# Turning one of seven 128-row units of each batch on VectorE and by DMAs instead of on TensorE

## What is computed

```python
q = (text_hidden @ Wq).reshape(B, T_text, 16, 128).transpose(0, 2, 1, 3)
k = (vision_tokens @ Wk)...; v = (vision_tokens @ Wv)...     # 8 key/value heads, each used twice
scores = jnp.einsum('bhtd,bhsd->bhts', q, k) / sqrt(128)
attn = jax.nn.softmax(jnp.where(mask, scores, -jnp.inf), axis=-1)
out = jnp.einsum('bhts,bhsd->bhtd', attn, v)
x = layernorm(x + out.transpose(0, 2, 1, 3).reshape(B, T_text, -1) @ Wo)
```

## Time and profile before

| | us |
|---|---|
| median of 3 runs | 1717.02 |
| lowest and highest | 1716.77, 1717.21 |
| span of the profiled execution | 1718.6 |
| busy PE, DVE, ACT, POOL in it | 1685.0, 1221.3, 937.2, 664.6 |
| mean granted clock of PE | 0.994 |

### The profile page before, as it was taken

The page is one execution under the profiler, slowest core; times in us unless marked ns, Lnnn a source line. Parts: engine busy times, 40 slices in busy tenths (PEclk is TensorE's granted clock), DMA queues, the critical chain, the costliest instruction groups (busy, mean ns, idle before and its releaser), DMA issues.

```text
span 1718.6 us, 28903 instructions
## 1 busy us (share of the span) xinstructions
PE 1685.0 (98%) x10034; PEld 1517.0 (88%) x10034; DVE 1221.3 (71%) x3377; ACT 937.2 (55%) x1717; POOL 664.6 (39%) x417
## 2 busy tenths in 40 slices
PE   7999999999999999999999999999999999999996
PEld 7998889898989898989898989989898989888985
DVE  5655676877787878777778777776878787756557
ACT  5444465656565656565656565565656565644543
POOL 1220344525243333333334343443525341355435
PEclk9999999999999999999999999999999999999998
DMA  5234643423141423333232323232324130431433
GB/s 197 81 132 130 193 95 78 70 68 81 54 97 41 90 44 88 48 86 68 62 68 63 68 63 68 70 66 77 74 61 89 52 57 12 112 114 40 121 90 95
DMA packets 102856, 140.29 MB, mean 82 GB/s; under 512 B 37022, under 2 KB 81728, under 8 KB 102592
## 3 DMA queue, kind: packets, MB, share of 16 engines
q1 hardware_dynamic: 60784, 115.47, 26.8%
q10 hardware_dynamic: 38912, 14.80, 4.0%
q0 software_dynamic: 3024, 8.26, 1.8%
HBM read 113.62 MB, written 24.89 MB: 81 GB/s over the span
## 4 chain that ended last, share of the span: by engine, by line
PE 93%; DVE 2%; issue 1%; ACT 1%; DMA 1%; POOL 0%; another core or an unknown queue 0%; POOLq 0%; SPq 0%; ACTq 0%; DVEq 0%
PE b_turn L831 17%; PE b_out L850 9%; PE b_out L851 9%; PE b_out L852 9%; PE b_score L817 9%; PE b_score L819 9%; PE b_score L818 9%; PE b_out L860 5%; PE a_bank L344 5%; PE c_gate L1513 2%; PE c_down L1540 1%; PE a_bank L370 1%; PE a_bank L395 1%; PE a_bank L424 1%; PE a_bank L417 1%
## 5 line engine op out<-in xcount | busy, mean ns | idle before, releaser
L895 ACT CAST b_pT_hi<-b_turn 125x512 fp32r<-125x512 f32 (+1 forms) x768 | 406.8, 530 | 543.0 <-PE b_turn L831 539.8
L997 DVE TENSOR_TENSOR b_pT_lo<-b_turn,b_pT_hi 125x512 fp32r<-125x512 f32 (+1 forms) x768 | 478.0, 623 | 259.7 <-ACT b_pT_hi L895 254.2
L983 DVE CUSTOM_DVE_ANT_0 b_p<-b_score,b_mask_add 128x500 f32<-128x500 f32 x672 | 451.9, 673 | 58.9 <-PE b_turn L831 24.4
L831 PEld LDWEIGHTS b_turn<-ident,b_p 128*125 128x125 f32 x2688 | 409.4, 186 | 55.2
L831 PE MATMUL b_turn<-ident,b_p 128*125 128x128 f32 x2688 | 418.1, 272 | 0.0
L901 ACT ACTIVATE b_p<-b_p,b_shift 128x1500 f32<-128x1500 f32 x224 | 347.5, 1551 | 2.1 <-DVE b_top_min L991 2.1
L850 PE MATMUL b_out<-b_pT_hi,b_c_hi 125*128 125x512 f32 (+1 forms) x768 | 346.5, 451 | 0.7 <-DVE b_pT_lo L997 0.6
L1135 POOL TENSOR_TENSOR b_oT_lo<-b_oT,b_oT_hi 128x896 fp32r<-128x896 f32 x32 | 67.6, 2112 | 624.5 <-ACT b_oT_hi L925 588.0
L851 PE MATMUL b_out<-b_pT_lo,b_c_hi 125*128 125x512 f32 (+1 forms) x768 | 280.9, 366 | 0.0
L852 PE MATMUL b_out<-b_pT_hi,b_c_lo 125*128 125x512 f32 (+1 forms) x768 | 280.5, 365 | 0.0
L817 PE MATMUL b_score<-b_cT_hi,b_q_hi 128*128 128x500 f32 x672 | 262.9, 391 | 0.0
(11 more groups left out here) (250 smaller groups left out, 2402.1 us busy)
## 6 DMA issues: line engine op xcount, KB each, us to landing
cT_in<-in_ctxT SPq DMA_DIRECT2D x32, 750.0 KB, 9.8
b_c_in<-in_ctx SPq DMA_DIRECT2D x32, 750.0 KB
q_store<-a_fold_in_or_q_stage SPq DMA_DIRECT2D x16, 896.0 KB, 4.2
q_in<-q_store SPq DMA_DIRECT2D x32, 448.0 KB, 7.1
b_rden_all<-rden_store ACTq DMA_DIRECT2D x32, 256.0 KB, 3.6
b_rden_all<-rden_store ACTq DMA_DIRECT2D x32, 192.0 KB, 3.7
b_mask_in<-in_mask SPq DMA_DIRECT2D x32, 187.5 KB, 9.4
slot_store<-c_y2T SPq DMA_DIRECT2D x35, 128.0 KB, 1.7
```

The costliest lines, as they stand in the source:

```text
L831: mm = pe.transpose(turn_bank[n % 3][0:CK, u * 128:(u + 1) * 128], p[slot % 2][:, u, c * CK:(c + 1) * CK], ident[:])
L895: act.copy(pT_hi[:, n % 3, 0:w], turn_bank[n % 3][0:CK, 0:w]).then_inc(hi_done, 1)
L983: dve.tensor_tensor_reduce(out=p[slot % 2][:, u, keys], in0=score_bank[j][:, 0:FW], in1=mask_add[:, b, keys], scale=1.0, scalar=-3.0e38, o ...
L997: dve.tensor_tensor(pT_lo[:, n % 3, 0:w], turn_bank[n % 3][0:CK, 0:w], pT_hi[:, n % 3, 0:w].bitcast(F32), ALU.subtract).then_inc(lo_done, 1)
```

## The change

In every even slot the first unit is no longer transposed by PE. In step 5 of the slot, once its exponential is done, DVE turns it in 32x32 blocks with one instruction, `turn_blocks`: out of `p` (128 rows x 1500 keys, seen as 4 x 12 blocks of 32 columns; a chunk of 125 keys is taken as 4 x 32, and four columns of padding are added) into a new tile, `by_block`. SP then issues 16 DMAs of 32 partitions x 384 floats, `move_blocks`, that put the blocks at their partitions in `keyed`. `p_round` copies the high part of the unit's 128 columns from `keyed`, before it waits for PE, and that of the other 384 from PSUM. `p_rest` subtracts in two instructions likewise, the first of which has both inputs in SBUF. `scores` waits for `turned` from the second unit of an even slot on.

To make room, `oT_lo` is written over `oT` and `c_lo` over the raw values: `c_in` goes, `c_raw` has a place for each batch of the pair, and its load waits for `pv_done` itself. SP's loads are written out instead of looped and stand in another order around the moves. At the start of `phase_c` the loads of `y2` wait for other things, and two pairs of semaphores are merged.

```diff
+QUADS = 4
+ACROSS = 32 * CH
+ROW_PAD = 4
...
+        def written_over(name, shape, dt):
+
+            return nc.alloc_sbuf_tensor_at(f"b_{name}_over", shape, dt, offset=edge[name])
...
+        oT_lo = written_over("oT", [128, XH, 2, S], F32R)
         oT_hi = sb("oT_hi", [128, XH, 2, S], F32R)
-        oT_lo = sb("oT_lo", [128, XH, 2, S], F32R)
...
+        by_block = sb("by_block", [128, QUADS, CH, 32])
...
-        c_in = sb("c_in", [CK, CH * CD])
+        keyed = sb("keyed", [128, QUADS, ACROSS])
         c_hi = sb("c_hi", [CK, 2, CH * CD], F32R)
-        c_lo = sb("c_lo", [CK, 2, CH * CD], F32R)
+        c_raw = sb("c_raw", [CK, 2, CH * CD])
+        c_lo = written_over("c_raw", [CK, 2, CH * CD], F32R)
...
-        p[0] = sb("p0", [128, UNITS[0], CTX])
+        p[0] = sb("p0", [128, UNITS[0], CTX + ROW_PAD])
...
+        BLOCKS_AT = 5
+        MOVES = 16 * QUADS * QUADS
...
+        def keyed_chunk(c):
+            return keyed[0:CK, :, 32 * c:32 * (c + 1)]
+
+        def by_blocks(ap):
+            return ap.rearrange("p (a j) -> p a j", j=32)
...
+            def load_values(i, b):
+                n = 2 * i + b
+                if n >= 2:
+                    sp.wait_ge(pv_done, 2 * CH * (n - 1))
+                if n:
+                    sp.wait_ge(c_loaded, 16 * n)
+                sp.dma_start(c_raw[:, b, :], D["ctx"][n]).then_inc(c_loaded, 16)
+
+            def move_blocks(i, b):
+
+
+                n = 2 * i + b
+                if n:
+                    sp.wait_ge(lo_done, CH * (2 * n - 1))
+                sp.wait_ge(blocks_turned, n + 1)
+                for a in range(QUADS):
+                    for r in range(QUADS):
+                        sp.dma_start(keyed[32 * r:32 * (r + 1), a, :],
+                                     by_block[32 * a:32 * (a + 1), r].rearrange("q c j -> q (c j)")).then_inc(
+                                         keyed_loaded, 16)
...
-            def loads(i, first=False):
-                load_q(i, 0)
-                load_scores(i, 0)
-                load_values(i, 0)
-                load_q(i, 1)
-                load_scores(i, 1)
-                if not first:
-                    store(i - 2)
-                residual(i - 1)
-                load_values(i, 1)
-
-            loads(1, first=True)
-            with sp.Fori(2, NPAIR) as i:
-                loads(i)
-            store(NPAIR - 2)
-            residual(NPAIR - 1)
+            for i in range(NPAIR):
+                move_blocks(i, 0)
+                if i < END:
+                    load_q(i + 1, 0)
+                    load_cT(i + 1, 0)
+                    load_mask(i + 1, 0)
+                if i:
+                    load_values(i, 1)
+                if i < END:
+                    load_q(i + 1, 1)
+                    load_cT(i + 1, 1)
+                move_blocks(i, 1)
+                if i < END:
+                    load_mask(i + 1, 1)
+                if i:
+                    store(i - 1)
+                residual(i)
+                if i < END:
+                    load_values(i + 1, 0)
...
-                for u in range(units(slot)):
+                for u in range(1 - slot % 2, units(slot)):
...
-                g, w = STEPS * i + n, 128 * units(n // CH)
-                act.wait_ge(turned, g + 1)
+                g, slot, c, w = STEPS * i + n, n // CH, n % CH, 128 * units(n // CH)
+                own = 128 * (1 - slot % 2)
                 if not (first and n < 3):
                     act.wait_ge(pv_done, g - 2)
-                act.copy(pT_hi[:, n % 3, 0:w], turn_bank[n % 3][0:CK, 0:w]).then_inc(hi_done, 1)
+                if own:
+                    if c == 0:
+                        act.wait_ge(keyed_loaded, MOVES * (2 * i + slot // 2 + 1))
+                    act.copy(by_blocks(pT_hi[:, n % 3, 0:own]), keyed_chunk(c))
+                act.wait_ge(turned, g + 1)
+                act.copy(pT_hi[:, n % 3, own:w], turn_bank[n % 3][0:CK, own:w]).then_inc(hi_done, 1)
...
-                if u == 0 and not (first and slot < 2):
+                if u == 1 - slot % 2 and not (first and slot < 2):
...
+            def turn_blocks(i, slot):
+
+
+                n = 2 * i + slot // 2
+                dve.wait_ge(exp_done, PUNITS * i + unit0[slot] + 1)
+                if n:
+                    dve.wait_ge(keyed_loaded, MOVES * n)
+                own = p[0][:, 0, :]
+                keys = bass.AP(own.tensor, own.offset, [own.ap[0], [32, QUADS], [CK, CH], [1, 32]])
+                dve.transpose(by_block[:], keys).then_inc(blocks_turned, 1)
+
             def p_rest(i, n):
-                w = 128 * units(n // CH)
+                slot, c, w = n // CH, n % CH, 128 * units(n // CH)
+                own = 128 * (1 - slot % 2)
                 dve.wait_ge(hi_done, STEPS * i + n + 1)
-                dve.tensor_tensor(pT_lo[:, n % 3, 0:w], turn_bank[n % 3][0:CK, 0:w],
-                                  pT_hi[:, n % 3, 0:w].bitcast(F32), ALU.subtract).then_inc(lo_done, 1)
+                if own:
+                    dve.tensor_tensor(by_blocks(pT_lo[:, n % 3, 0:own]), keyed_chunk(c),
+                                      by_blocks(pT_hi[:, n % 3, 0:own]).bitcast(F32), ALU.subtract)
+                dve.tensor_tensor(pT_lo[:, n % 3, own:w], turn_bank[n % 3][0:CK, own:w],
+                                  pT_hi[:, n % 3, own:w].bitcast(F32), ALU.subtract).then_inc(lo_done, 1)
...
+                    if n // CH % 2 == 0 and n % CH == BLOCKS_AT:
+                        turn_blocks(i, n // CH)
...
-            sp.wait_ge(*attention.c_split)
+            sp.wait_ge(*attention.first_batch_weighed)
+            load_y2(2)
+            sp.wait_ge(*attention.keyed_taken)
             load_y2(0)
-            sp.wait_ge(*attention.first_batch_weighed)
             load_y2(1)
-            load_y2(2)
```

81 lines of the change are left out of this document (40 added, 41 removed).

## The result

The changed kernel takes **1843.06 us** (median of 4; 1840.93 to 1846.43), the kernel before 1717.12: ratio **1.0733**, 95% interval 1.0718 to 1.0748. The forecast was 1772.6 with a range up to 1830. The direction was right, the size was not: 126 us came on top where the sum had 56, and the time lies 13 us above the range.

What follows compares the result with a forecast made beforehand. PE was taken to bound the kernel, with 93% of the chain. 1718.6 - 43.4 (transposes) + 98 (waits for GpSimd) + 1 (tail) = 1774.2 us profiled, less 1.6: 1772.6 us; range 1690 to 1830.

Steps and rivals of the forecast that it cites:

- What is removed: PE's queue: 384 transposes fewer at 0.113 us each, a gain of 43.4 us, all on PE.
- ScalarE: 384 added casts of 125x128 out of SBUF, 0.15 to 0.3 us each, hidden by the wait for PE: 0 us.
- VectorE's block transpose: One 1536-column instruction behind step 5's low part: 1.75 us, bounds 0.9 and 3.5, just fitting, not waiting for GpSimd.
- The wait for GpSimd: Low-part pieces with both inputs in SBUF wait for GpSimd's present instruction: 98 us, bounds 45 and 135.
- the walk: Steps 15 to 26 and 39 to 50 followed against GpSimd's instructions: with block-transpose lateness, 6.5 us for each of 15 pairs.
- The moves: SyncE's sixteen DMAs per batch land in time for ScalarE's cast: 0 us, upper end 1 us in each of 32 batches.
- The tail: The load of the first y2 tiles is issued later, at 1490.3 instead of 1473.5: +1 us (0 to 5).
- C: Rival: moves come late or the block transpose takes two passes, 30 to 56 us on top; 0.16 with the stalls' upper end.
- A: Rival: VectorE's pieces do not wait for GpSimd or always slip in between, 1675 us; chance 0.14.
- B: Rival: GpSimd's blocks exist but VectorE makes them up, 1 to 2.7 us a pair, 1690 to 1715 us; chance 0.08.
- the ring: Follow-up theory: late moves delay ScalarE's denominators' store, whose landing delays exponentials and VectorE's next block transpose, enlarging each lateness.

Runs made afterwards that it cites:

- e8: Changed kernel with four large moves per batch, low part's first operand from PSUM, moves ahead of the loads and the opening's last store (wrong numbers): 1680.5 us, ratio 0.9781.
- e5: Changed kernel with block transposes and sixteen moves that nobody reads, TensorE making all four transposes: 1725.4 us, ratio 1.0035.
- h2: Changed kernel with VectorE copying moved blocks into PSUM before one low part, moves ahead of the loads, block transpose at step 4: 1745.6 us, ratio 1.0159.
- e1: Changed kernel with the first operand of the seventh unit's low part from PSUM instead of SBUF (wrong numbers): 1758.2 us, ratio 1.0248.
- h1: e8 with sixteen moves per batch again in place of four (wrong numbers still): 1762.7 us, ratio 1.0272.
- f0: Changed kernel with SyncE's order alone changed: moves ahead of the q and ctxT loads and the opening's last store: 1861.7 us, ratio 1.0816.
- e6: Kernel before with only the low part split in two, the 128-column piece having both inputs in SBUF (wrong numbers): 1825.1 us, ratio 1.0627.
- e3: Changed kernel with four large moves per batch and the low part's first operand from PSUM, old order (wrong numbers): 1744.5 us, ratio 1.0160.
- e2: Changed kernel with four large moves per batch in place of sixteen (wrong numbers): 1787.3 us, ratio 1.0418.
- e9: Changed kernel with moves ahead of the loads and ScalarE copying moved blocks into PSUM for one 512-column low part: 1767.8 us, ratio 1.0307.
- f1: e9 with the block transpose one step earlier, at step 4 of the slot: 1729.0 us, ratio 1.0057.

## Why the prediction was right in direction and wrong in size

**What is removed: right.** 2304 transposes at an unchanged mean of 272 ns. The sum had -43.4; e8 has -37. The 6 us between are of the size of what e5 shows for layout, loads, block transposes and traffic together (7.8 us, with sixteen moves); no run parts them further.

**ScalarE: right.** The new cast takes 295 ns (estimate 150 to 300) and in e8 nobody waits for it.

**VectorE's block transpose: right.** 1.77 us (estimate 1.75), 1767 to 1771 ns all 32 times; 27 of the 32 ran beside a GpSimd instruction. The Trainium skill ("SBUF — State Buffer", Who interferes with whom) has it that an instruction with at most one SBUF input outside the two-port modes stays out of the contention: with h2's copy (282 to 297 ns 384 times) the traces agree.

**The wait for GpSimd: right in mechanism, the size in part by luck.** The sum had 98 us. Four pairs of runs measure it: 85 (e1 to the changed kernel), 99 (h1 to f0), 107 (e6, of which 13 fall in the first pair, which the walk left out), and only 43 where four moves come late by their place (e3 to e2). The mechanism is the one in the earlier trace rows. The places in the walk were partly others. In the changed kernel's timeline a piece begins inside `oT_lo` 31 times, inside `q_lo` 30 times and inside `c_lo` 29 times in 32 batches, 14 of these in steps 15 to 26, where the walk had it fall into the projection; inside `cT_lo` only 3 times, where the walk had 1.7 us a pair; and 15 times inside a short instruction (L1176) that the walk did not have. One error made up for the other.

**The moves: this step failed.** It took 0, with 1 us in each of 32 batches as its upper end. The runs show 78 us for the moves as they stand in the changed kernel (e8 to e1). Three things went wrong in it. (1) An issue was priced at 0.57 us from the earlier trace rows, where four stood alone; sixteen take 10.02 to 10.56, and with 1.9 to 3.6 us for the last landing the blocks are there 12 to 13 us after the transpose. The working had 10.9 to 13.4 itself, against 11.5, and let PE's 1.6 us of lead pay for the difference. It doesn't: ScalarE waits in all 32 batches, and 1.7 us of more lead won 39 us where GpSimd's wait was out of the way (e9 to f1). (2) The working saw that the second batch's moves stand behind a load that takes 11.3 us, and let them arrive by 980.5 to 983, where the cast stands at 981.06. For the place it was right by the cover of the issues: with sixteen the place costs nothing (e1 and h1), with four it cost 64 (e3 to e8). The two faults hide each other, and removing one shows the other. (3) The first batch was not walked at all. Its moves stand behind the opening's last store, the wait is 15.0 us, and the first pair as a whole ended 24 us late, 18.5 of them without the pair in SBUF too (e1).

**The tail: +1 forecast, -2 measured.** Nothing rests on it.

**The rivals.** C had the mechanism (moves late, ScalarE waits for `b_keyed`) and was priced at 30 to 56 us on top, 1800 to 1830. It was the case that came true, and higher: 1843. In the changed kernel the two stalls come on top of one another, 78 and 85 us, which no rival had at full size; the upper end of C should have been made from both late batches and the first one. That they add here is no rule: beside four moves the pair cost 43. A and B fell with e6: there the period of a pair rises from 81.2 to 87.4 us by the piece, 6.2 us where the walk had 6.5.

**What stays open.** Moves that are some 2 us late per batch (ScalarE's waits for them are 1.5 us a batch in h1) cost 2.6 us a batch in the span (82 us over 32), of which the clock is 0.3 by the estimate above (13 less 5 over 32). Cutting the ring through the store gained nothing, but not in a clean test; another path, VectorE coming late to the next block transpose, is in the chain but was not isolated. Why the pair in SBUF costs half as much beside four late moves is open too.

## What to carry to other kernels

A gain on the engine that sets the pace can be lost several times over to one new instruction a step with both inputs in SBUF beside a busy GpSimd: look at where both inputs of each new instruction lie before counting columns. Price a group of small DMAs as one long occupation of the queue that issues them, add what stands ahead of it in each place where it occurs, the very first one included, and compare with the lead only after all other claims on that lead. Where two delays lie one over the other, remove both before judging either, and put each back alone: here the place in the queue cost 64 us or nothing, and the number of moves 14 or 82, depending on the other.

## What the hardware showed that I had not expected

- A VectorE instruction of 292 ns took up to 3.41 us with both inputs in SBUF beside GpSimd, the same subtraction with one input in PSUM 278 to 293 (e1), and a copy of the same columns with its one input in SBUF 282 to 297 (h2). The piece with both in SBUF was worth 107 us (e6).
- A move of 48 KB takes SyncE 0.63 us with its gap, but single issues took up to 3.7 us (4.4 in f0); its landing is 1.9 us after the issue at the least (2.8 in the median). A move of 192 KB, issued 2.3 us behind a load of 750 KB and as the last of four, landed after 11.1 us (e3).
- After 4.8 us without work TensorE ran 4.4 us at a granted clock of 0.50 (f0), so a long stall is paid again in part when it is over; the changed kernel, whose waits before L889 are 2.3 us at most from 414 to 1119 us, showed 1.00 there.
